# A decoder kernel on one core: two of three parts of a lower half on VectorE, the last 512 columns on GpSimd

## The reference

```python
def _L0_xattn_ref(x, latents, gamma_media, beta_media, gamma_lat, beta_lat, Wq, bq, Wkv, bkv, Wo, bo):
    ...
    xn = _layernorm(x, gamma_media, beta_media)
    ln = _layernorm(latents, gamma_lat, beta_lat)
    q = ln @ Wq + bq
    kv_input = jnp.concatenate([xn, ln], axis=1)
    kv = kv_input @ Wkv + bkv
    k, v = jnp.split(kv, 2, axis=-1)
    ...
    q = q * DH ** (-0.5)
    sim = jnp.einsum('bhid,bhjd->bhij', q, k)
    attn = jax.nn.softmax(sim, axis=-1)
    out = jnp.einsum('bhij,bhjd->bhid', attn, v)
    out = out.transpose(0, 2, 1, 3).reshape(b, -1, INNER)
    return out @ Wo + bo
```

## Time and profile before

| | us |
|---|---|
| median of 3 runs | 2020.86 (2019.73 to 2023.51) |
| the profiled execution | 2022.75 |
| its span in the trace | 2020.9 |
| TensorE busy | 1824.7 (90%) |
| VectorE busy | 1625.7 (80%) |
| ScalarE busy | 1278.7 (63%) |
| GpSimd busy | 235.5 (12%) |
| mean granted clock | 0.984 |

### The profile page before, as it was taken

One profiled execution on the slowest core, in us unless ns is written; L12 is line 12 of the kernel. 1 busy time (PEld: TensorE's weight loads), 2 busy tenths in 40 slices (PEclk: granted clock), 3 DMA queues, 4 the chain that ended last, 5 costly groups with the idle time before them and its releaser, 6 DMA issues.

```text
span 2020.9 us, 41783 instructions
## 1 busy us (share of the span) xinstructions
PE 1824.7 (90%) x17100; PEld 1026.7 (51%) x17100; DVE 1625.7 (80%) x2631; ACT 1278.7 (63%) x1915; POOL 235.5 (12%) x250
## 2 busy tenths in 40 slices
PE   4999988989899997989999998898989999798987
PEld 3677753322567773232457775332256777323235
DVE  8888878698788877789688887869778887878954
ACT  6666645569566655738756664556956665573852
POOL 1000001120200001030210000112020000103514
PEclk8999999999999999999999999999999999999999
DMA  7466630000266660001136663000025666000226
GB/s 315 83 129 129 127 84 13 9 28 23 59 128 126 128 130 23 6 18 40 32 94 126 127 133 76 13 9 27 23 61 127 125 128 129 25 6 18 91 69 129
DMA packets 450765, 159.92 MB, mean 79 GB/s; under 512 B 426213, under 2 KB 441840, under 8 KB 450064
## 3 DMA queue, kind: packets, MB, share of 16 engines
q1 hardware_dynamic: 444880, 147.78, 32.6%
q0 software_dynamic: 2384, 6.36, 0.9%
q10 hardware_dynamic: 3312, 3.11, 0.7%
HBM read 33.96 MB, written 9.47 MB: 21 GB/s over the span
## 4 chain that ended last, share of the span: by engine, by line
PE 58%; DVE 30%; ACT 5%; issue 4%; DMA 3%; POOL 0%; ACTq 0%; POOLq 0%; DVEq 0%
DVE nmx L2322 15%; PE ps L807 10%; PE ps L809 9%; PE ps L808 9%; PE ps L1191 6%; PE ps L979 4%; PE ps L973 4%; PE ps L974 4%; PE ps L1177 3%; DMA arena<-arena 2%; PE ps L1141 1%; DVE arena L2130 1%; DVE st L1950 1%; PE ps L1258 1%; PE ps L1201 1%
## 5 line engine op out<-in xcount | busy, mean ns | idle before, releaser
L2322 DVE TENSOR_REDUCE nmx<-ps 128x2 f32<-128x1024 f32 x384 | 444.7, 1219 | 14.5 <-PE ps L1141 13.0
L1770 ACT ACTIVATE arena<-ps 128x512 f32<-128x512 f32 x768 | 407.0, 601 | 51.5 <-PE ps L1177 46.5
L2115 DVE TENSOR_SCALAR_CACHE_REDUCE ps<-ps 128x1536 f32<-128x1536 f32 x128 | 225.7, 1764 | 40.3 <-PE ps L809 39.7
L1191 PE MATMUL ps<-arena 128*17 128x256 f32 x3072 | 240.8, 389 | 0.0
L2130 DVE SCALAR_TENSOR_TENSOR arena<-arena,rs 128x1536 f16<-128x1536 f32 x128 | 231.6, 1810 | 4.2 <-ACT arena L1660 4.2
L1660 ACT ACTIVATE arena<-arena,rs 128x1536 f16<-128x1536 f32 x128 | 200.8, 1569 | 42.9 <-DVE rs L2121 42.9
L1651 ACT ACTIVATE arena<-ps,nm 128x1536 f32<-128x1536 f32 x128 | 197.0, 1539 | 8.9 <-DVE ps L2115 8.9
L973 PE MATMUL ps<-arena 128*128 128x128 f16 x1536 | 185.3, 219 | 1.3 <-DMA arena<-arena 1.3
L974 PE MATMUL ps<-arena 128*128 128x128 f16 x1536 | 185.3, 219 | 0.0
L807 PE MATMUL ps<-arena 128*128 128x512 f16 (+2 forms) x508 | 174.5, 347 | 8.2 <-DMA arena<-zx_d 6.4
L809 PE MATMUL ps<-arena 128*128 128x512 f16 (+2 forms) x508 | 174.4, 347 | 0.0
(11 more groups left out here) (355 smaller groups left out, 3502.0 us busy)
## 6 DMA issues: line engine op xcount, KB each, us to landing
arena<-in_weights SPq DMA_DIRECT2D x8, 929.0 KB, 23.0
arena<-arena SPq DMA_DIRECT2D x72, 64.0 KB, 2.1
arena<-arena SPq DMA_TRANSPOSE x268, 3.2
arena<-in_ctx SPq DMA_DIRECT2D x4, 1024.0 KB, 5.4
arena<-in_ctx_t SPq DMA_DIRECT2D x4, 1024.0 KB, 4.9
arena<-in_experts SPq DMA_DIRECT2D x1, 3840.0 KB, 11.6
arena<-zx_d ACTq DMA_DIRECT2D x23, 132.0 KB
arena<-arena SPq DMA_DIRECT2D x72, 32.0 KB, 1.9
```

What stands on the lines that cost most here:

```text
L1191: mm(ps[32 * j:32 * j + VW, 7, cols], v17[:, kt, 4 * g_ + j, :], pr_[:, (4 * t + j) % RING, cols], start=(kt + half == 0), stop=(kt == mod ...
L1770: A(pr_[:, n % RING, :], ps[:, 4 + n % 3, :], ACT.Exp).then_inc(b_exp.sem, 1)
L2115: TS_(s_, s_, -XS, None, ALU.mult, ALU.min, accum_out=nm[:, i:i + 1]).then_inc(s_max.sem, 1)
L2322: V.tensor_reduce(nmx[:, g_ % 2, ch, :, pp, i], ps[:, 2 * (z % 2):2 * (z % 2) + 2, :], AX.X, ALU.max, negate=True)\
```

## The change

GpSimd makes the lower half of the columns 1024 to 1535 in two operations: it multiplies `xp` by `rs` in place, then subtracts the upper half. VectorE's operation covers the columns 0 to 1023. A new semaphore, `s_lo_end`, counts GpSimd's operations, two for a tile. The transpose of the lower half and the exponential that overwrites `xp` wait for it as well.

```diff
+        LO_CUT = 1024
...
             def transpose_lo(b, n, s_):
                 sp.wait_ge(s_lo.sem, s_lo.at(b, n + 1))
+                sp.wait_ge(s_lo_end.sem, s_lo_end.at(b, 2 * n + 2))
                 sp.dma_start_transpose(xpT[s_][1], xq[s_][1]).then_inc(tl_in[s_].sem, 16)
...
+            def scaled_lo_end(b, n):
+
+                i = n % NT
+                pool.wait_ge(s_hi.sem, s_hi.at(b, n + 1))
+                if n >= 2:
+                    pool.wait_ge(tl_in[i % 2].sem, tl_in[i % 2].at(b, 16 * (n // 2)))
+                else:
+                    pool.wait_ge(*((zx_out.sem, zx_out.at(b, 0)) if b else (pad_out.sem, 16 * (1 + NE))))
+                at = slice(LO_CUT, NKV)
+                full, hi, lo = xp[:, i % 2, at], xq[i % 2][0][:, at], xq[i % 2][1][:, at]
+                nc.gpsimd.tensor_tensor(full, full, rs[:, i:i + 1].to_broadcast([P, NKV - LO_CUT]), ALU.mult).then_inc(s_lo_end.sem, 1)
+                pool.wait_ge(s_lo_end.sem, s_lo_end.at(b, 2 * n + 1))
+                nc.gpsimd.tensor_tensor(lo, full, hi, ALU.subtract).then_inc(s_lo_end.sem, 1)
...
-                    if k == 0 and b:
-                        scatter_rows(b - 1)
+                    if k == 0:
+                        if b:
+                            scatter_rows(b - 1)
+                        for n in range(NTI):
+                            scaled_lo_end(b, n)
...
                 if reused:
                     act.wait_ge(s_lo.sem, s_lo.at(b, n - 1))
+                    act.wait_ge(s_lo_end.sem, s_lo_end.at(b, 2 * n - 2))
...
-                STT(xq[i % 2][1], xp[:, i % 2, :], rs[:, i:i + 1], xq[i % 2][0], ALU.mult, ALU.subtract).then_inc(s_lo.sem, 1)
+                at = slice(0, LO_CUT)
+                STT(xq[i % 2][1][:, at], xp[:, i % 2, at], rs[:, i:i + 1], xq[i % 2][0][:, at], ALU.mult, ALU.subtract).then_inc(s_lo.sem, 1)
```

More of the change, by code:

```diff
@@ L352, in decoder @@
         s_mm, s_max, s_exp, s_rs = sig("s_mm", NTI), sig("s_max", NTI), sig("s_exp", NTI), sig("s_rs", NTI)
-        s_hi, s_lo = sig("s_hi", NTI), sig("s_lo", NTI)
+        s_hi, s_lo, s_lo_end = sig("s_hi", NTI), sig("s_lo", NTI), sig("s_lo_end", 2 * NTI)
         th_in, tl_in = ([sig(f"{n_}{k}", 16 * NTI // 2) for k in range(2)] for n_ in ("th_in", "tl_in"))
```

## The result

| | us |
|---|---|
| before, median of 7 runs | 2021.28 (2019.73 to 2023.78) |
| after, median of 7 runs | 2028.35 (2027.39 to 2031.58) |
| after / before | 1.0035, 95% interval 1.0025 to 1.0046 |
| profiled execution after, its span | 2031.58, 2029.8 |
| mean granted clock, profiled before, after | 0.984, 0.978 |

What follows compares the result with a forecast made beforehand. TensorE bounds the kernel, so only its waits at the first tile and last head count. First tile +0.4 and last head +0.7 gave +1.1 us on the median 2020.86: 2022.0, range 2017.0 to 2027.0.

Steps and rivals of the forecast that it cites:

- what it adds: GpSimd's multiply (1.27 us) and subtract (1.16) for each tile, the pair done 2.58 us after the upper half; 311 us in all.
- a dearer multiply: Reason given for part of the slower chance (0.25): a longer GpSimd multiply would add to first tile and tile 29.
- First tile: Tile 0 of each block: 0.53 us gained at the split returns as a transpose wait; +0.09 a block, +0.4 in all.
- rival 3: First tile and tiles 29 to 31: GpSimd's subtract goes ahead of waiting VectorE; +6.6 us, 2027.5; chance 0.17.
- it decides from the grant order at the first tile: Rival 3's sign: the first tile's lower half on VectorE starts at 77.07 and lasts over 2 us.
- The overlap price: Wherever VectorE and GpSimd operations overlap on SBUF, whoever comes second pays the overlap less 0.14 us.
- rival 2: Full blocking between the engines: +0.29 at the first tile, +0.64 at tile 29; +3.1 us, 2024.0; chance 0.15.
- Regular tiles: The 28 tiles before the last head: 0.12 us of overlap, nothing to pay, TensorE does not wait.
- Last head: Tiles 28 to 31: tile 27's gain given back, tile 29's transpose +0.31 us in three blocks; together +0.7.
- its -0.2: Last head of the fourth block, which lacks the tile 29 wait: taken as -0.2 us.
- the delay falls each time on the reciprocal: Rival 3, tiles 29 to 31: VectorE's delay passes to the next tile's upper half, 0.5 to 1.5 us, taken as 1.0.
- The cover of 0.3 us at tile 31: Last tile: the lower half's transpose lands at 270.8, TensorE wants it at 271.11, so no wait.

Runs made afterwards that it cites:

- d_order: The changed kernel, with GpSimd's subtract at tile 0 made to wait for VectorE's operation; 2028.43 us, ratio 1.0033 to the kernel before.
- k_full_operand: The changed kernel, with GpSimd's multiply reading a full second operand instead of the broadcast scale (computes something else); 2029.24 us, ratio 1.0035 to before.
- f_again: The changed kernel itself, run once more beside the kernel before; 2029.6 us, ratio 1.0035.
- c_middle: The changed kernel, with GpSimd working in tiles 1 to 27 only and VectorE making the whole lower half elsewhere; 2020.27 us, ratio 0.9996 to before.
- i_first_only: The kernel before, with GpSimd's share of the lower half at tile 0 of each block alone; 2024.7 us, ratio 1.0010.
- m_wait_short: The kernel before, with VectorE's lower half at tile 0 cut into 4 operations, no GpSimd; 2025.27 us, ratio 1.0012.
- g_reorder: The kernel before, with VectorE's lower half at tile 0 put ahead of the unit's split, no GpSimd; 2019.12 us, ratio 0.9984.
- h_best: GpSimd in tiles 1 to 27 only, plus VectorE's lower half ahead of the split at tile 0; run twice: 2017.74 and 2016.68 us, ratios 0.9977 and 0.9963 to before.
- j_last_only: The kernel before, with GpSimd's share of the lower half in the last head alone (tiles 28 to 31); 2025.3 us, ratio 1.0013.
- b_last: The changed kernel, with VectorE making the whole lower half in the last head (GpSimd in tiles 0 to 27); 2023.36 us, ratio 1.0005 to before.
- n_wait_long: The kernel before, with VectorE's lower half at tile 0 cut into 8 operations, no GpSimd; 2031.92 us, ratio 1.0044.
- e_cut1280: The changed kernel, with the split moved from column 1024 to 1280, so GpSimd makes 256 columns; 2021.42 us, ratio 0.9996 to before.

## Why the prediction was wrong

**The step that failed first** is in "what it adds": the multiply with a broadcast operand was in no row, the multiply of two full operands (L671, 1.268) was taken for it, and the trace after gives 1.04 for all 128. What a shorter multiply would do was never worked out; the only allowance was for "a dearer multiply". Yet the order hung on it: by the forecast's own times the subtract was ready at 77.20 with a multiply of 1.27, against VectorE's arrival at 77.07, a margin of 0.13. With 1.04 it is ready at 76.97, ahead. d_order, k_full_operand and the changed kernel show the two orders. By k_full_operand this step explains the order at the first tile, but not the missing 6 us; for these, three terms were too small or missing: the first tile in either order, the last head, and the clock; and a late transpose came in that no row showed.

**First tile.** Forecast +0.09 a block, a gain of 0.53 at the split given back at the transpose. Measured +0.35, with no gain first: VectorE pays 0.88 and saves 0.53. This is what rival 3 described (a lower half of over 2 us, "it decides from the grant order at the first tile"), with a price that was too high, 0.65 a block, since with the shorter multiply VectorE had only the subtract to wait out. But rival 3 had the subtract overtake a VectorE operation that was already waiting; in fact it was simply first. That rival 3's sum (2027.5) lies so near the result is luck: its two places were to cost 6.6 us and by the traces cost 2.8 to 3.8; the rest is the clock and the late transpose, for which it had no term. Even the forecast's own path was under-priced: k_full_operand shows a new wait of 0.80 for 0.6 and +0.44 a block for +0.09.

**The overlap price** (overlap less 0.14) held well enough, and against a full block (rival 2): 1.08 together cost VectorE 0.88. In the last head 1.00 together cost the subtract 0.85 (2.01 for 1.16).

**Regular tiles.** Right but for the multiply: 1.28, 1.04, 1.16, no wait, nothing gained or lost.

**Last head.** Forecast +0.7, measured +1.4 in the first profile and +2.4 in f_again. Block by block +0.31 was forecast for three and -0.2 for the fourth. In the first trace the three come to 0.87, for 0.93, and the error is the fourth, +0.57: its -0.2 was a guess with no working, and while the wait of 1.30 that the kernel before has there for an upper transpose went, waits of 0.52, 0.29 and 1.25 for transposes came. In f_again the second and third block are above the forecast too. That three blocks agree is in part luck, for a term was missing: tile 28. Tile 27 did gain what was said, in all blocks but the third (in the first the wait of 1.06 became 0.43, forecast 0.53). Timeline after, last head of the first block:

```profile
250.84 1.16 POOL L769 TENSOR_TENSOR arena<-arena 128x512 f16<-128x512 f32 x1
250.90 2.18 DVE L2151 SCALAR_TENSOR_TENSOR arena<-arena,rs 128x1024 f16<-128x1024 f32 x1
...
255.59 1.56 DVE L2151 SCALAR_TENSOR_TENSOR arena<-arena,rs 128x1024 f16<-128x1024 f32 x1
...
256.15 2.01 POOL L769 TENSOR_TENSOR arena<-arena 128x512 f16<-128x512 f32 x1
...
258.39 0.22 PE L992 MATMUL ps<-arena 128*128 128x128 f16 x1 [0.60 <-DMA arena<-arena]
...
259.43 2.17 DVE L2151 SCALAR_TENSOR_TENSOR arena<-arena,rs 128x1024 f16<-128x1024 f32 x1
...
259.47 1.04 POOL L767 TENSOR_TENSOR arena<-arena,rs 128x512 f32<-128x512 f32 x1 [1.31 <-ACT arena L1680]
260.59 2.01 POOL L769 TENSOR_TENSOR arena<-arena 128x512 f16<-128x512 f32 x1
...
263.30 0.84 PE L998 MATMUL ps<-arena 128*128 128x128 f16 x12 [1.45 <-DMA arena<-arena]
```

Without a unit to split, VectorE comes to the lower half sooner after the upper one, at tile 28 already (250.90), meets the subtract and ends 0.9 late; the reciprocal behind it, and with it the upper half of tile 29, slip by 0.25. A wait for an upper transpose appears (0.60) that wasn't there; 0.34 of it is in c_middle as well, where VectorE makes all of tile 28: there the gain of tile 27 is given back, as forecast. The rest is tile 28's. The other order is no better here either: in k_full_operand VectorE is undisturbed at tile 28 (1.28), the subtract pays (2.13), and the last heads lose as much. Tile 29 then is about as forecast (1.56 and 2.01, forecast 1.63 and 2.09), its transpose is issued 0.31 later as forecast, and the wait of 1.49 is 1.45. Rival 3 had this chain too ("the delay falls each time on the reciprocal"), for tiles 29 to 31. The cover of 0.3 us at tile 31 held in the changed kernel; in the first block of k_full_operand it did not (a wait of 0.60).

**The clock** had no term at all. The forecast treated a longer wait of TensorE as worth its own length. By the count above a wait of 2.12 instead of 1.77 brings a fall in about 11 of 24 places, 4 x 1.7 x 11/24 = 3.1 us an execution. That is an estimate from profiled executions; i_first_only and m_wait_short, at 1.4 and 1.6 us of added waiting, came out 2.5 us over before, which leaves the clock about 1 us there, and the mean granted clock of the 11 executions of m_wait_short (0.983) is that of before in its series.

**The fourth block's transpose** was not foreseeable from the rows of before. In c_middle, too, TensorE waits 1.04 us for it. The DMA view of c_middle from 1515.9 to 1522 us (40 slices of 0.15 us):

```profile
GB/s 0 0 0 0 0 0 0 22 218 290 292 285 290 289 294 290 260 155 0 0 151 269 270 153 13 10 10 10 10 260 289 294 287 289 264 0 0 0 0 0
...
q1 hardware_dynamic: 3136, 0.79, 75.8%
q8 instruction: 1, 0.02, 1.0%
```

Five slices at about 10 GB/s stand in the middle of the transposes, with one packet of the kind "instruction". In 13 of the 17 traces such a packet falls 0.7 to 2.7 us behind the issue of this transpose, and in all 13 it takes 4.5 to 5.2 us to land; in the other four it lands after 3.2 or 3.3. Of these, the kernel before has the packet 4.2 us ahead of the issue; in g_reorder and the two of h_best it comes 2.7 to 2.8 us behind, and the transpose after this one takes 3.4 to 3.8 instead. m_wait_short and j_last_only are among the 13, with no GpSimd work at that tile and waits of 1.05 and 1.18. In b_last, i_first_only and n_wait_long the transpose is as late, but TensorE had been slowed by a stretch at half clock and came no earlier. So it goes by where the packet falls, not by the split. That the packet is the cause is argued, not shown: no run took it away.

**The sum of what was measured**, for the changed kernel: first tile 4 x 0.35 = 1.4, last heads 1.4 to 2.4, the late transpose 1.2, the clock behind the first tile 1.7 in one trace and 3.4 in the other: 5.7 to 8.4, around the 7.1 of the medians. Forecast had been 1.1. The late transpose and the clock are counted from profiled executions, and c_middle and e_cut1280 have the late transpose too and lose nothing, so the split of the 7.1 is an estimate. What stays open is why the clock falls behind some of the waits and not behind others of the same length, and how often it does in executions that have no trace. The rest of the clock's difference between the two profiled executions (0.984 and 0.978) lies between the latent stages and wasn't tied to the change: 3.4 of the 8.9 us between the first two spans arose there, and in f_again -1.2 of 7.5.

## What to carry to other kernels

Work moved to an idle engine isn't free when both engines read the same memory: place the pair in time first, at each of the few spots where the busiest engine waits, and ask there who is first; a duration that is taken from a similar row has to be bounded on both sides when an order hangs on a tenth of a microsecond. Keep the split out of those spots (here tiles 0 and 28 to 31) and no cost could be measured (0.9996); a clear gain, 3.5 and 6.1 us, came only together with a better order at the first tile. A wait of TensorE that grows from 1.8 to over 2.1 us can cost more than its growth, since the clock may fall at it.

## What the runs showed of the hardware

- GpSimd's multiply of 128x512 float32 by a column broadcast along the row takes 1.04 us, with two full operands 1.27; by 256 columns 0.61, and the subtract 0.67 where 512 columns take 1.16.
- VectorE's operation with two SBUF inputs and a GpSimd one hardly run together: 1.08 us of overlap cost the later one 0.88, and 0.98 in k_full_operand (2.14 for 1.16). Where VectorE's record began 0.040 to 0.045 us ahead of GpSimd's, VectorE paid (57 of 57); where it began 0.051 or 0.052 ahead, GpSimd did (3 of 3), and likewise at 0.150 to 0.171 (8 of 8, k_full_operand).
- Cutting one VectorE operation of 1536 columns (1.81 us) into 4 makes it 2.19, into 8 it is 2.71: 0.13 us a cut.
- TensorE's clock fell to half for 3.4 us at 11 of the 24 waits of 2.1 to 2.7 us at the first tile, and at none of the 44 of 1.2 to 1.8 (one of these places has a fall behind a second wait, of 2.50), whether GpSimd had a part in the wait or not.
- One packet of the kind "instruction" in a run of transposes goes with about 0.8 us at 10 GB/s in their traffic (290 before and after), and one of them lands after 4.5 to 5.2 us instead of 3.2.
